# Gated attention: the values' bias added by DVE on the way out of PSUM, and the values projected between the two halves of the gate

## What is computed

```python
h = x * rsqrt(mean(x*x) + EPS) * norm_scale
uv = silu(h @ W1 + b1)                       # W1: 128 x 640
u, v, base = split(uv, [256, 512])           # gate, values, base
q, k = base * gamma[0] + beta[0], base * gamma[1] + beta[1]
qk = rope(einsum('bnd,bmd->bnm', q, k) / 128)
kernel = square(relu(qk))
out = u * einsum('bnm,bme->bne', kernel, v)
return out @ W2 + b2 + shortcut
```

## Time and profile before

| | us |
|---|---|
| median of 3 runs | 1698.32 |
| the runs | 1694.06, 1701.26, 1698.32 |
| the profiled execution | 1694.06 |
| its span | 1692.3 |

### The profile page before, as it was taken

How to read it: one execution, slowest core, us unless ns; L and a number is a source line. 1 busy time by engine, 2 the same in 40 slices (tenths; PEclk the granted TensorE clock), 3 DMA queues, 4 the chain that set the end, 5 groups by cost and what they waited for, 6 DMA issues and landing times. The chain is left out here.

```text
span 1692.3 us, 27305 instructions
## 1 busy us (share of the span) xinstructions
PE 1313.1 (78%) x8747; PEld 922.6 (55%) x8747; DVE 1006.4 (59%) x1912; ACT 786.4 (46%) x1420; POOL 869.9 (51%) x880
## 2 busy tenths in 40 slices
PE   5679999999984431487662784888889888999997
PEld 3567777777752320376552563333333357877775
DVE  2765555555537776221111488888888566667886
ACT  3224444444443421232220345787877567664443
POOL 1454445444431004488886532777677045745766
PEclk9889999999996556699996687999999999999999
DMA  5061000000001012444444400000000121233443
GB/s 176 1 246 72 0 0 0 0 0 0 0 0 27 0 38 70 91 94 80 84 84 99 139 1 2 2 2 0 0 0 1 65 96 51 91 100 46 53 62 40
DMA packets 84440, 80.92 MB, mean 48 GB/s; under 512 B 18266, under 2 KB 73016, under 8 KB 82960
## 3 DMA queue, kind: packets, MB, share of 16 engines
q1 hardware_dynamic: 56163, 59.44, 11.0%
q0 software_dynamic: 26176, 19.40, 8.3%
q10 hardware_dynamic: 2016, 1.00, 0.2%
HBM read 46.23 MB, written 39.64 MB: 51 GB/s over the span
## 5 line engine op out<-in xcount | busy, mean ns | idle before, releaser
L1953 PE MATMUL at_slot<-at_qm,at_ks 128*128 128x512 bf16 (+1 forms) x640 | 160.4, 384 | 19.4 <-DVE at_clip L2158 10.2
L2822 POOL DMA_INDIRECT out_h<-ff_tokens x70 | 109.0, 1558 | 74.6 <-DVE ff_tokens L2875 56.0
L509 PE MATMUL ga_kv<-ga_kern,ga_v 128*128 128x274 f32 x512 | 133.5, 403 | 13.5 <-ACT ga_kern L598 12.6
L2037 ACT ACTIVATE at_clip<-at_slot,at_four 128x1024 bf16<-128x1024 f32 (+1 forms) x96 | 106.8, 1113 | 32.1 <-PE at_slot L1953 30.3
L1436 POOL DMA_INDIRECT moe_sums<-ex_y,slot_sums x69 | 108.4, 1571 | 22.2 <-issue 21.3
L2158 DVE TENSOR_SCALAR at_clip<-at_slot 128x1024 bf16<-128x1024 f32 (+1 forms) x96 | 116.1, 1217 | 3.0 <-PE at_slot L1953 2.7
L660 POOL TENSOR_TENSOR ga_rot<-ga_by_cos,ga_by_sin 128x274 f32<-128x274 f32 x64 | 48.6, 759 | 134.8 <-DVE ga_by_sin L704 134.8
L509 PEld LDWEIGHTS ga_kv<-ga_kern,ga_v 128*128 128x128 f32 x512 | 92.2, 189 | 37.8 <-ACT ga_kern L598 16.8
L2812 POOL DMA_INDIRECT by_group<-mx_stage,mx_place_i x69 | 72.2, 1046 | 48.7 <-ACT mx_stage L2698 27.9
L1526 DVE TENSOR_SCALAR ex_share<-ex_rows,owner_sb 128x1 f32<-128x1 f32 x31 | 6.6, 214 | 147.6 <-PE ex_ps_y L1478 147.6
L590 ACT ACTIVATE ga_rot<-ga_rot 128x274 f32<-128x274 f32 x128 | 53.4, 429 | 84.6 <-POOL ga_rot L660 75.2
(11 more groups left out here) (481 smaller groups left out, 3881.2 us busy)
## 6 DMA issues: line engine op xcount, KB each, us to landing
moe_sums<-ga_zeros SPq DMA_DIRECT2D x8, 1152.0 KB, 13.4
ar_rows<-moe_sums SPq DMA_DIRECT2D x34, 256.0 KB, 3.8
ex_down<-in_down SPq DMA_DIRECT2D x32, 192.0 KB, 2.6
by_group<-in_blank SPq DMA_DIRECT2D x1, 4655.0 KB, 19.9
ff_tokens<-by_group SPq DMA_DIRECT2D x17, 266.0 KB, 3.1
token_rows<-ct_rows SPq DMA_DIRECT2D x17, 256.0 KB, 2.4
out_h<-mx_rows SPq DMA_DIRECT2D x22, 192.0 KB, 2.1
H<-in_text SPq DMA_DIRECT2D x1, 4096.0 KB, 21.4
```

The source lines that it names most:

```text
L509: last = nc.tensor.matmul(kv[:, e, 0:HALF], v[p][:, mt + 2 * side, e * P:(e + 1) * P], kern[(p + g) % 2][:, side, :], start=mt == 0 and si ...
L1953: last = nc.tensor.matmul(to[r0:r0 + r, g % 2, :].rearrange("p (s n) -> p s n", s=2), ks[m][:, t * P:t * P + r], qm[m][:, 2 * g:2 * g + 2, ...
L2037: nc.scalar.activation(to[0:r], of[0:r], ACT.Relu, bias=four[0:r], scale=-1.0).then_inc(by_act, 1)
L2822: nc.gpsimd.indirect_dma_start(out=out, out_offset=bass.IndirectOffsetOnAxis(ap=ids, axis=0), in_=R[j % RING], in_offset=None, bounds_chec ...
```

## The change

The values' bias leaves the DRAM round trip and TensorE. It is loaded as a 128 x 256 float32 table, one more constant on ACT's queue, and DVE adds it while moving the values from `misc` to a new SBUF tile (`v_pre`, `v_pre_tail`), on which ACT then applies the silu. In every engine the whole values of a batch are now handled between the gate halves: TensorE projects them in unit 3 and gate half 1 in unit 4. `misc` is now passed on from gate half 0 to the values (`u_sb`), to gate half 1 (`v_biased`), to the tail values (`u_sb`), to the base (`v_biased`). ACT takes the tail values' silu behind the kernel of unit 1 instead of ahead of it. On DVE the addition of the whole values stands in unit 3 behind `low_of` and ahead of the rotation of the next batch's unit 0, and that of the tail values in unit 0 behind the rotation of unit 1 and ahead of `tokens_low`.

```diff
@@ load_inputs
-                  ("ident", "ident"), ("W1", "W1"), ("W2", "W2"), ("same_expert", "same_expert"),
+                  ("ident", "ident"), ("b1_v", "b1_v"), ("W1", "W1"), ("W2", "W2"), ("same_expert", "same_expert"),
...
-                sp.dma_start(k["b1_v3"][r, :], parts_d[part:part + 1, NE:BIAS_ROWS, :].rearrange("o e d -> o (e d)")).then_inc(laid, 16)
-            sp.wait_ge(laid, 144)
+            sp.wait_ge(laid, 96)
...
-            nc.vector.memset(k["b1_v3"][:], 0.0)
@@ gated_attention, tensor
             def project_u(b, p, e):
                 if e == 0:
                     pe.wait_ge(base_sb, b + 1)
                 else:
-                    pe.wait_ge(u_sb, 2 * b + 1)
+                    pe.wait_ge(v_biased, 2 * b + 1)
...
             def project_v(b, p, tails):
                 if tails:
-                    pe.wait_ge(v_sb, 2 * b + 1)
+                    pe.wait_ge(u_sb, 2 * b + 2)
...
                 else:
-                    pe.wait_ge(u_sb, 2 * b + 2)
+                    pe.wait_ge(u_sb, 2 * b + 1)
...
-                    split_matmul(nc, out, tokens, [w[:, EXPAND:2 * EXPAND] for w in W1p], True, False)
-                    last = nc.tensor.matmul(out, k["ones_bf"][:, 0:rows], k["b1_v3"][:], start=False, stop=True)
+                    last = split_matmul(nc, out, tokens, [w[:, EXPAND:2 * EXPAND] for w in W1p], True, True)
...
                     if g == 1 and not final:
-                        pe.wait_ge(v_sb, 2 * b + 2)
+                        pe.wait_ge(v_biased, 2 * b + 2)
                         project_base(b + 1, 1 - p)
                     weigh(b, p, g, first)
                     if g == 3 and not final:
-                        project_u(b + 1, 1 - p, 1)
+                        project_v(b + 1, 1 - p, False)
...
                     if g == 4 and not final:
-                        project_v(b + 1, 1 - p, False)
+                        project_u(b + 1, 1 - p, 1)
@@ scalar
             def v_out(b, p, tails, first=False):
-                act.wait_ge(v_ps, 2 * b + tails + 1)
+                act.wait_ge(v_biased, 2 * b + tails + 1)
...
-                    last = nc.scalar.activation(v[p][:, 0:4, :], misc[:].rearrange("p b (s n) -> p (b s) n", s=2), ACT.Silu)
+                    last = nc.scalar.activation(v[p][:, 0:4, :], v_pre[:], ACT.Silu)
                 else:
-                    last = nc.scalar.activation(v[p][0:TAILS, 4, :], misc[0:TAILS, 0, 0:EXPAND], ACT.Silu)
+                    last = nc.scalar.activation(v[p][0:TAILS, 4, :], v_pre_tail[0:TAILS], ACT.Silu)
...
-                    if g == 0:
-                        v_out(b, p, True, first)
                     if g < UNITS - 1:
                         kernel_of(b, p, g + 1, first and g == 0)
                     elif not final:
                         kernel_of(b + 1, 1 - p, 0)
+                    if g == 0:
+                        v_out(b, p, True, first)
...
-                    if g in (2, 3):
-                        u_out(b + 1, 1 - p, g - 2, first)
+                    if g == 2:
+                        u_out(b + 1, 1 - p, 0, first)
                     if g == 4:
                         v_out(b + 1, 1 - p, False, first)
+                        u_out(b + 1, 1 - p, 1, first)
@@ vector
+            def bias_v(b, tails, first=False):
+                dve.wait_ge(v_ps, 2 * b + tails + 1)
+                if not first:
+                    dve.wait_ge(v_sb, 2 * b)
+                if not tails:
+                    nc.vector.tensor_tensor(v_pre[:], misc[:].rearrange("p b (s n) -> p (b s) n", s=2),
+                                            k["b1_v"][:].unsqueeze(1).broadcast_to([P, 4, EXPAND]), ALU.add).then_inc(v_biased, 1)
+                else:
+                    nc.vector.tensor_tensor(v_pre_tail[0:TAILS], misc[0:TAILS, 0, 0:EXPAND], k["b1_v"][0:TAILS], ALU.add).then_inc(v_biased, 1)
...
+                    if g == 0:
+                        bias_v(b, True, first)
                     if g == 0 and not final:
                         tokens_low(b + 1, 1 - p)
...
+                    if g == 3 and not final:
+                        bias_v(b + 1, False)
...
             low_of(0, 0, 1)
+            bias_v(0, False, True)
             nc.vector.memset(zeros[:], 0.0).then_inc(zeros_set, 1)
```

More of the change, by code:

```diff
@@ L58 @@
 NOWHERE = 1 << 20
-BIAS_ROWS = NE + EXPAND // P
+BIAS_ROWS = NE
 COLS = {}
@@ L370, in gated_attention @@
         v = [sb(f"v{p}", [P, 5, EXPAND]) for p in range(2)]
+        v_pre = sb("v_pre", [P, 4, EXPAND])
+        v_pre_tail = sb("v_pre_tail", [2 * GAP, EXPAND])
         by_cos = [sb(f"by_cos{p}", [P, 2, HALF]) for p in range(2)]
@@ L386, in gated_attention @@
         met, hs_low, qk_low, w_cut = sem("met"), sem("hs_low"), sem("qk_low"), sem("w_cut")
+        v_biased = sem("v_biased")
         tail0, tail = MTILES[2]
@@ L544, in _ @@
             project_u(0, 0, 0)
+            project_v(0, 0, False)
             project_u(0, 0, 1)
-            project_v(0, 0, False)
             score(0, 0, 0, True)
@@ L612, in units @@
                         base_out(b + 1)
-                    if g in (2, 3):
-                        u_out(b + 1, 1 - p, g - 2, first)
+                    if g == 2:
+                        u_out(b + 1, 1 - p, 0, first)
                     if g == 4:
                         v_out(b + 1, 1 - p, False, first)
+                        u_out(b + 1, 1 - p, 1, first)
             base_out(0, True)
             u_out(0, 0, 0, True)
+            v_out(0, 0, False, True)
             u_out(0, 0, 1, True)
-            v_out(0, 0, False, True)
             kernel_of(0, 0, 0, True)
@@ L2985, in build @@
              "pick_wide": sb("pick_wide", [P, NGRP, 2, P], F32R),
-             "cols": sb("cols_sb", [P, NCOLS]), "ident": sb("ident_sb", [P, P]), "ones_bf": sb("ones_bf", [P, P], BF16), "b1_v3": sb("b1_v3", [P, EXPAND], BF16),
+             "cols": sb("cols_sb", [P, NCOLS]), "ident": sb("ident_sb", [P, P]), "ones_bf": sb("ones_bf", [P, P], BF16), "b1_v": sb("b1_v_sb", [P, EXPAND]),
              "down_b3": sb("down_b3", [P, NE * P], BF16),
@@ L3024, in _arrays @@
     b1 = np.asarray(inp["L0_attn_b1"])
-    a["bias_rows"] = np.concatenate([np.asarray(inp["L0_ffn_b_down"]), b1[EXPAND:2 * EXPAND].reshape(-1, P)], 0)
+    a["bias_rows"] = np.asarray(inp["L0_ffn_b_down"])
+    a["b1_v"] = np.broadcast_to(b1[EXPAND:2 * EXPAND], (P, EXPAND))
     a["router"] = np.asarray(inp["L0_ffn_W_router"])
```

## The result

The changed kernel takes 1675.12 us (median of 4 runs, 1670.29 to 1677.24), the kernel before, on the same chip, 1697.88 (4 runs, 1694.06 to 1701.26). The ratio is 0.986 [0.983, 0.989]: faster by 22.8 us, with a forecast of 25.7 and a time forecast of 1672.6. The profiled execution took 1674.66 us with a span of 1672.8, against a span of 1692.3 before: 19.5 us less. Each kernel of this text was profiled once on its chip. The stage behind the attention starts at 458.39 instead of 477.87, 19.48 us earlier, so all of it lies where the change was made.

The account below looks back on a forecast made before the run. TensorE was taken as nearly full (328 of 350 us). Savings of 23.7 (fourteen laps) + 1.4 (first lap) + 0.3 (ahead of the loop) + 0.3 (loading) = 25.7 us gave 1672.6 us, range 1664 to 1684.

Parts of the forecast that it names:

- The order: TensorE, each lap: gate half 1 (0.75 us) takes the place of the values with bias (1.85 us), saving 1.10.
- Tail bias product: TensorE, tail values: dropping the bias product saves 0.30 us a lap, bounds 0.12 and 0.36.
- The wait ahead of the tail values: TensorE waiting for `misc` before the tail values: 0.59 us falls to 0.30, saving 0.29 a lap.
- part A: Lap from tail weighting's end to last weighting, 5.71 us; twelve value products there add 0.72, fit in 1.16 idle, cost nothing.
- The paragraph on what comes late next: Checked base projection, tail's silu and GpSimd against a lap 1.69 us shorter: no cost, each within 0.2 us of costing.
- rival 2: GpSimd holds DVE's new addition up to 2.75 us; only 4 us gained, 1694 us; chance 0.04.
- part B: The lap's other 17.18 us: TensorE's own issue plus a 0.59 us wait; forecast 1.69 us shorter.
- Loading: Loading stage: three transfers less on SP's queue, 0.29 us each, against 0.5 us for the added table; net 0.3 saved.
- What ACT reads: ACT's silu of the values, now reading SBUF instead of PSUM: taken as 1.02 less 0.05 us.
- Rival 1: Only the eighty bias products' own time is gained, 10 to 13 us, as other waits close up: 1686 us; chance 0.14.
- Rivals 2 and 3: Rival 2 has its line; the other: slower, addition beyond 2.75 us delays unit 0's rotation, 1712 us at 4.0; chance 0.03.
- Rival 4: The change does nothing, as the chain of part A would span the whole lap: 1698 us; chance 0.04.

Follow-up runs that it names:

- the kernel with the order alone: Kernel before with values projected between the gate halves, bias kept as a product; ratio 0.9889 to the kernel before, lap 21.63 us.
- The eight pieces: Changed kernel with the whole values' addition cut into eight of 128 columns: ratio 0.9891 to the kernel before; also with the later query remainder: 0.9868.
- the later query remainder: Changed kernel with DVE's query remainder moved behind the rotation of unit 4, next to the key's; ratio 0.9829 to the kernel before, lap 20.97 us.

## Why the prediction held, and which step was off

**The order (1.10 a lap): right.** Measured 1.09 (1.85 less 0.76), and the kernel with the order alone shows that it carries the lap. *Tail bias product (0.30, bounds 0.12 and 0.36): right*, 0.32 in the timeline and 0.18 to 0.25 between kernels that differ in it.

**The wait ahead of the tail values (0.29): near in size, for another reason.** It fell by 0.38, not by 0.29. The forecast let the addition push the rotation, square and both silus; the gate's silu would have waited for the values' silu. It waits for TensorE (0.43 us idle). The last weighting and all behind it came 0.45 later than forecast, and this gave the chain the slack. The eight pieces show both: they cost nothing here, and 0.28 once part A is short.

**Part A at no cost: this is the step that failed.** "Cost nothing; what hides it is the chain" was true of TensorE's twelve products, and the chain was taken at its old length. It grew by 0.45, as DVE's query remainder, a link of it, fell beside GpSimd's key. The paragraph on what comes late next asked only which of GpSimd's *results* TensorE would wait for, and found 0.2 us to spare. It did not ask which DVE instruction would now run beside which of GpSimd's. The row that shows the price was there: the remainder at 1.62 us. The forecast used it for the new addition alone (rival 2), where it does not hold: the addition, one operand of which is in PSUM, took 1.22 to 1.23 us in each kernel. With the remainder moved out of the chain, part A went from 6.16 to 5.56, and in the laps in which it got ahead of GpSimd by itself part A was 5.72.

**The signs.** Of those that were to show the forecast, the lap of 21.1 to 21.3 us was missed (21.62, under the 21.8 that would have refuted it). So were two that hang on part A: the wait for the last weighting stayed at 0.80 by the prediction's way of counting (0.3 to 0.5 forecast), and the scores of unit 0 still wait for the key's remainder, by 0.12 instead of 0.38. The value products at 1.73 are just above their range. And one sign of being wrong came true: the base waits for the token remainder, which the forecast gave 0.2 us to spare. The token remainder stands behind GpSimd and so did not move up with TensorE. It costs the lap nothing that can be told, since the kernel with the order alone has no such wait and the same lap.

**The sum.** Steady laps: forecast 14 x 1.69 = 23.7; measured 18.0 (320.45 us from the second tail-values product to the last, now 302.45), 1.29 a lap. Of the 5.7 us that are missing, 14 x (0.45 - 0.11) = 4.8 are part A's growth less what part B gave beyond its forecast, as one lap shows them; the rest is that every second lap is 0.12 to 0.16 longer than that one. First lap: 1.48 against 1.4. Ahead of it, 0.46 up to the first tail values: from the first projection to the scores 0.31 against 0.3; DVE's addition stalled TensorE 1.32 us against about 1.6. Loading: 0.3 saved was the forecast, 0.87 lost at the block's start is the reading, within the scatter of that start. Behind the last tail values: 0.41 gained where the forecast had nothing, though the last batch too drops the bias product of its tail. In sum 18.0 + 1.5 + 0.5 - 0.9 + 0.4 = 19.5 against 25.7. That the median came within 2.5 us of the forecast is luck in part: the medians differ by 3.3 us more than the profiled executions. The lower bound of the addition was worked out wrongly, too: the slope between 0.409 us for 256 columns and 1.220 for 1024 gives 1.08 us for 1024 columns, not 0.81, which is the difference itself. It entered only the low end of the range.

**What ACT reads.** The silu of 1024 columns took 1.05 us from SBUF here and 1.06 with the addition in the old order, 1.02 from PSUM before and 1.00 in the kernel with the order alone. The forecast's 0.05 less was wrong in sign. The Trainium skill (VectorE: DVE Perf Modes, on the TRN2 errata) was right: 52 cycles more by its table, which I estimate at 0.04 us, and these rows agree with 0.03 to 0.06.

**The rivals.** Rival 1 (products' own time only) gives the gain to the products; in fact dropping them in favour of DVE's addition gave nothing without the order, and the order alone gave everything. Rivals 2 and 3 needed an addition of 2.75 us and more, and it took 1.22. Rival 4 had no change at all, and the lap fell by 1.30.

## What to carry to other kernels

A stretch made shorter on one engine slides the others against each other: list which DVE instructions with two SBUF operands will then lie beside GpSimd's, and price those at the end of GpSimd's instruction plus nearly their own time (here 0.58 us of 0.72). Put such an instruction behind the last one that the critical chain needs; the same edit is worth little before a change and much after it, so try it again after each. Before pricing what is taken off an engine, follow the waits from one place in the lap to the same place in the next: what is not on that closed path counts for nothing. Taking products off a nearly full engine gave nothing where they stood beside another engine's chain: here the order, which costs no work at all, was the gain.

## What the runs showed of the chip

An instruction of DVE with two SBUF operands that falls into one of GpSimd's does not slow down in proportion: in these rows it ends a fixed time behind GpSimd's end. Query remainder in the change: 297.69, which is 0.58 behind GpSimd's 297.11. In the kernel with the order alone: 297.53, where GpSimd's row of that kernel is

```profile
295.41 1.54 POOL L649 TENSOR_SCALAR ga_k<-ga_base,cols_sb 128x548 f32<-128x548 f32 x2
```

and so ends at 296.95, again 0.58 ahead. In the first batch before the change, the remainder ended at 124.43, 0.57 behind GpSimd's end at 123.86:

```profile
122.31 1.55 POOL L647 TENSOR_SCALAR ga_k<-ga_base,cols_sb 128x548 f32<-128x548 f32 x2
```

With the later query remainder it goes both ways: GpSimd's first sum ends at 294.06, the key's remainder (issued at 293.45) at 294.61, GpSimd's second sum at 295.13, each some 0.5 to 0.6 behind the one before it, where each takes 0.66 to 0.68 alone. Gate and rotations, with one operand in PSUM, kept 0.71 to 0.73 beside the same instructions of GpSimd. The Trainium skill (SBUF — State Buffer, the section on SBUF's two separate sides) says that of such a DVE instruction and one of GpSimd's the one that starts first holds the shared ports for its whole length while the other waits. These rows agree, in both directions: in the lap at 361.76 GpSimd is held for 0.58 us instead. Where the two start within 0.1 us of each other the rows don't say who will win: 0.07 behind GpSimd's start the remainder got ahead at 361.76 and was held at 318.52. In the prediction I had read such a row as a factor on the duration. One thing more stands in the earlier trace rows: the remainder was issued at 122.81, inside the first of GpSimd's two key instructions, which ended at 123.11, and yet it was held until behind the second. So a DVE instruction that waits did not get in between two that follow each other on GpSimd.

Eight DVE additions of 128 columns took 1.67 us together, one of 1024 took 1.22: 0.45 us more for seven more instructions, back to back.
